# Graph attention with routed experts: the feed-forward and routing stage written out without a loop, weight splitting moved to POOL in the attention

## What is computed

```
hs = layer_norm(_layernorm(x)); ht = layer_norm(h_target)
q = (ht @ Wq + bq) / sqrt(32); k = hs @ Wk + bk; v = hs @ Wv + bv      # 8 heads
logits = where(adj != 0, q @ k.T, -1e30); probs = softmax(logits)
ht = layer_norm(ht + (probs @ v) @ Wo + bo)
x = x + ht + gelu(ht @ W1) @ W2                                          # W1: 256x1024
xn = _layernorm(x); gate_logits = xn @ gate_w.T
vals, idx = top_k(gate_logits, 2); topk_w = softmax(vals)
for e in range(8):                                                       # 8 experts, 256->1024->256
    x += comb[:, e:e+1] * (gelu(xn @ w1[e].T + b1[e]) @ w2[e].T + b2[e])
```

## Time and profile before

| What | Value |
|---|---|
| Median of 3 runs (lowest, highest) | 1286.0 us (1283.02, 1286.46) |
| The profiled execution: time, span | 1281.83 us, 1279.9 us |
| Mean granted clock of TensorE, share of full speed | 0.903 |
| Busy, share of the span: PE, ACT, DVE, POOL | 81%, 63%, 63%, 14% |
| Moved by DMA | 128.71 MB, mean 101 GB/s |

### The profile page before, as it was taken

How to read it: one execution, slowest core, us unless ns; L and a number is a source line. 1 busy time by engine, 2 the same in 40 slices (tenths; PEclk the granted TensorE clock), 3 DMA queues, 4 the chain that set the end, 5 groups by cost and what they waited for, 6 DMA issues and landing times. The chain is left out here.

```text
span 1279.9 us, 25331 instructions
## 1 busy us (share of the span) xinstructions
PE 1030.5 (81%) x7150; PEld 638.6 (50%) x7151; DVE 802.6 (63%) x2186; ACT 804.0 (63%) x975; POOL 181.0 (14%) x163
## 2 busy tenths in 40 slices
PE   4926699989999899989999258558612899999994
PEld 2612244444444444444444135345411788888984
DVE  7718477867787677867787268838851534433442
ACT  4514599989999899889988125325402655555552
POOL 6400000000000000000000121331241122222221
PEclk9965699999999999999999569969955999999997
DMA  5693313311151113211240734253235232333323
GB/s 173 155 317 109 119 51 117 116 44 40 50 178 51 50 51 113 97 52 50 86 145 29 260 105 165 80 185 135 85 110 187 80 52 51 51 51 51 51 49 84
DMA packets 84561, 128.71 MB, mean 101 GB/s; under 512 B 16283, under 2 KB 59043, under 8 KB 81731
## 3 DMA queue, kind: packets, MB, share of 16 engines
q1 hardware_dynamic: 71954, 115.06, 27.9%
q0 software_dynamic: 8656, 11.29, 5.3%
q10 hardware_dynamic: 3856, 1.19, 0.4%
HBM read 96.82 MB, written 26.23 MB: 96 GB/s over the span
## 5 line engine op out<-in xcount | busy, mean ns | idle before, releaser
L597 DVE CUSTOM_DVE_ANT_0 masked<-ps,maskA 128x512 f32<-128x512 f32 x544 | 366.4, 690 | 125.4 <-PE ps L699 105.2
L699 PE MATMUL ps<-ks,qs 96*128 96x512 f32 x544 | 267.2, 533 | 62.0 <-DVE piecemax L597 28.9
L652 ACT ACTIVATE masked<-masked,negmax 128x2048 f32<-128x2048 f32 x135 | 270.4, 2003 | 53.5 <-DVE negmax L603 50.1
L677 ACT ACTIVATE weights<-ps 128x1024 f32<-128x1024 f32 x256 | 254.0, 1015 | 38.4 <-PE ps L721 35.8
L719 PE MATMUL ps<-qs,ks 98*128 98x512 f32 x514 | 234.6, 515 | 6.7 <-DMA qs<-shift_lo 3.4
L721 PE MATMUL ps<-maskB,identb 128*128 (+1 forms) x514 | 205.1, 399 | 0.0
L699 PEld LDWEIGHTS ps<-ks,qs 96*128 96x128 f32 x544 | 109.4, 201 | 137.6 <-DVE piecemax L597 78.0
L1643 DVE TENSOR_TENSOR gT<-wall,gT 128x2048 f16<-128x2048 f32 x25 | 57.3, 2293 | 148.6 <-ACT gT L1697 148.6
L1736 PE MATMUL ps<-xT,wall 128*128 128x256 f16 x1200 | 139.7, 278 | 9.8 <-DVE xT L1634 9.8
L731 PE MATMUL ps<-weights,v_all 128*32 128x256 f32 x2048 | 137.1, 385 | 0.0
L1736 PEld LDWEIGHTS ps<-xT,wall 128*128 x1200 | 119.1, 100 | 26.5 <-issue 10.4
(11 more groups left out here) (178 smaller groups left out, 1046.4 us busy)
## 6 DMA issues: line engine op xcount, KB each, us to landing
adjA<-in_adj SPq DMA_DIRECT2D x20, 1024.0 KB, 5.9
adjB<-in_adjT SPq DMA_DIRECT2D x40, 512.0 KB, 4.1
wst<-in_w1T SPq DMA_DIRECT2D x8, 1024.0 KB, 4.8
wst<-in_w2T SPq DMA_DIRECT2D x8, 1024.0 KB, 5.6
xr<-expert_rows SPq DMA_DIRECT2D x26, 272.0 KB
qs<-q_high SPq DMA_DIRECT2D x70, 64.0 KB, 2.0
ks<-kq_hi SPq DMA_DIRECT2D x32, 128.0 KB, 2.3
wall<-ctx_cols SPq DMA_DIRECT2D x6, 512.0 KB
```

The lines of the kernel that those rows point to most:

```text
L597: dve.tensor_tensor_reduce(masked[:, a % 2, k * 512:(k + 1) * 512], ps[:, u % 2, :], maskA[:, a, k * 512:(k + 1) * 512], 1.0, NO_EDGE, ALU ...
L652: act.activation(masked[:, a % 2, :], masked[:, a % 2, :], ACT.Exp, bias=negmax[:, h % 2, a:a + 1], accum_out=rowsum[:, h % 4, a:a + 1]).t ...
L677: act.activation(weights[:, j % 4, :, :], ps[:, 2 + 2 * (j % 2):4 + 2 * (j % 2), :], ACT.Exp).then_inc(weights_ready, 1)
L699: pe.matmul(ps[:, u % 2, :], qs[0:KR, h % 4, a * P:(a + 1) * P], ks[0:KR, h, k * 512:(k + 1) * 512], start=True, stop=True)\
```

## The change

- Block 1 also writes a table of padding rows (`pad_rows`) to memory, and issues the attention's first two mask loads (`adjA`) before its barrier.
- In the attention POOL now works. In each head's step it divides one context by its sums (`scale_context`, on 64x256), splits one quarter of a 256x1024 pair of weights with three operations on 128x1024 (`split`), stores the halves to memory (`split_weights`), loads the next quarter, and copies `pad_rows` two or three times into `expert_rows`, so that every expert's region is full of padding beforehand. DVE inverts the sums of each head (`invert_sums`, 128x4, at u = 8). SP stores these inverses (`store_sums`), loads them spread over partitions (`load_inv`), and stores the context (`store_context`) behind the shift, once POOL has scaled it.
- Block 3 is written out for its four blocks, with no loop. No float32 weights are split in it: the halves are loaded in sets (`load_set`). ACT applies the normalisations (`normalise`), POOL adds the bias of the projection to the rows ahead of time (`add_bias`), DVE works on 128x512 and 128x1024 at once, `hidden` runs over all eight f first, and `back` follows for two tiles of 128 rows at a time. The hidden layer has a buffer for each of two blocks. There is no padding at its end, and the sets of the last experts are loaded as their memory comes free.
- Block 4 splits no weights.

```diff
                     def store_context(n, b, h):
-                        wait_apart(sp, context_summed, n + 2)
+                        wait_apart(sp, context_scaled, n + 2)
...
                     def store_sums(n, h):
-                        wait_apart(sp, rowsum_ready, TPB * (n + 1))
-                        sp.dma_start(sums[:, bass.ds(n, 1), :], rowsum[:, h % 4, :]).then_inc(sums_out[h % 4], 16)
+                        wait_apart(sp, inv_ready, n + 1)
+                        sp.dma_start(inv_rows[bass.ds(n, 1), :].rearrange("o (a p) -> p (o a)", p=P),
+                                     rowsum[:, h % 4, :], allow_slow_non_contiguous=True).then_inc(sums_out[h % 4], 16)
+                    def load_inv(n, b, h):
+                        sp.wait_ge(sums_out[h % 4], 16 * (b * (H // 4) + h // 4 + 2))
+                        sp.wait_ge(context_scaled, n + 1)
...
+                    def split(i):
+                        wait_apart(pool, wch_in, 16 * i + 16)
+                        pool.tensor_scalar(wch[:, :], wch[:, :], WSCALE, None, ALU.mult).then_inc(wch_scaled, 1)
...
+                        pool.tensor_copy(whl[:, 0, :], wch[:, :]).then_inc(wch_split, 1)
...
+                        pool.tensor_tensor(whl[:, 1, :], wch[:, :], whl[:, 0, :], ALU.subtract).then_inc(wch_split, 1)
...
+                    with pool.Fori(0, NB) as b:
+                        for h in range(H):
+                            n = b * H + h
+                            if h:
+                                scale_context(n - 1, h - 1)
+                            split(n + 4)
+                            store_split(split_weights[bass.ds(e + 1, 1), h // 2 % 2, :, :, h % 2, :]
...
+                                load_expert(2 * b + (h + 1) // 4, h + 1)
...
+                            for i in range(2 * (h % 4), 2 * (h % 4) + (3 if h % 4 == 3 else 2)):
+                                prefill(bass.ds(e * REGION + i * PR, PR))
+                        scale_context(n, h)
...
+                            elif u == 8:
+                                invert_sums(n + 1, (h + 1) % 4)
...
-                        dve.wait_ge(g_high, FC * b + f + 1)
-                        dve.tensor_tensor(gT[:, 1, f % 2, :], g32[:, f % 2, :], gT[:, 0, f % 2, :], ALU.subtract)\
+                        dve.wait_ge(g_high, FC * b + f + 1)
+                        dve.tensor_tensor(gT[b % 2][:, 1, f, :], g32[:, f % 2, :], gT[b % 2][:, 0, f, :],
...
-                    for n in range(2):
-                        stage_high(act, 0, n)
-                    high_turned(0, 0)
+                    normalise_h(0)
+                    high_turned(0)
+                    normalise_h(1)
+                    normalise_h(2)
+                    for f in range(FC):
+                        hidden_high(0, f)
+                        if f == 5:
+                            normalise_h(3)
...
+                    scatter(0)
+                    row_factors(1, 2)
+                    scatter(1)
+                    row_factors(1, 3)
+                    scatter(2)
+                    scatter(3)
```

More of the change, by code:

```diff
@@ L91, in graph_attention_and_experts @@
         ks = sb("ks", [KR + 2, H, T], F32R, ph12)
+        adjA = sb("adjA", [P, 2, T], I32, ph12)
+        adj_t = adj.rearrange("(i p) s -> i p s", p=P)
+        adjA_in = [sem(f"adjA_in{i}") for i in range(2)]
         x_in = [sem(f"x_in{g}") for g in range(NG)]
@@ new lines, in scatter @@
+                    def scatter(b):
+                        pool.wait_ge(rows_ready, 2 * b + 2)
+                        pool.wait_ge(slots_ready, 2 * b + 2)
+                        for a in range(TPB):
+                            for k in range(TOPK):
+                                pool.indirect_dma_start(
+                                    out=expert_rows[:, :], in_=rows[:, b % 2, a, :], in_offset=None,
+                                    out_offset=bass.IndirectOffsetOnAxis(ap=slots[:, b % 2, k, a:a + 1], axis=0),
+                                    bounds_check=E * REGION - 1).then_inc(scattered[b % 2], 16)
@@ new lines, in _ @@
+                    pe.wait_ge(wo_in, 16)
+                    attention_out(0)
+                    attention_out(1)
+                    turn_h2(0)
+                    attention_out(2)
+                    pe.wait_ge(ffn_in, 32)
+                    hidden(0, 0)
+                    attention_out(3)
+                    for f in range(1, FC):
+                        hidden(0, f)
+                    turn_h2(1)
+                    for f in range(FC):
+                        hidden(1, f)
+                    back(0, 0)
@@ new lines, in _ @@
+                    back(0, 1)
+                    turn_h2(2)
+                    for f in range(FC):
+                        hidden(2, f)
+                    back(1, 0)
+                    turn_xn(0)
+                    back(1, 1)
+                    pe.wait_ge(gw_in, 16)
+                    gates(0)
+                    turn_h2(3)
+                    for f in range(FC):
+                        hidden(3, f)
+                        if f == 4:
+                            pe.wait_ge(c3_ready, 8)
+                            ranks(0)
@@ L1543, in graph_attention_and_experts @@
+                    back(2, 0)
+                    turn_xn(1)
+                    back(2, 1)
+                    gates(1)
+                    back(3, 0)
+                    ranks(1)
+                    back(3, 1)
+                    turn_xn(2)
+                    gates(2)
+                    ranks(2)
+                    turn_xn(3)
+                    gates(3)
+                    ranks(3)
         ph4 = ExitStack()
@@ L1704, in _ @@
                     middle(0, 0)
-                    for n in range(2):
-                        stage_high(act, LATE[1], n)
                     with act.Fori(0, NPAIR // 2) as jj:
```

960 lines of the change are left out of this document (465 added, 495 removed).

## The result

The changed kernel takes 1447.6 us (median of 4 runs, 1445.3 to 1459.5), the kernel before beside it 1286.2 (4 runs). The ratio is 1.128, interval 1.122 to 1.134. The profiled execution has a span of 1445.2 us against 1279.9. The forecast was 1224, with a range up to 1262: both the sign and the size were wrong.

A forecast was written before the change was run, and what follows sets the result against it. It took PE (539 of 578 us) and ACT (517) as close to full in the attention. -14 - 49 - 5.5 - 11.5 + 21.5 = -58.5 from 1281.83 gave 1223.3, forecast 1224 us; range 1198 to 1262.

The forecast's parts named there:

- The attention pays: Attention: what the change costs there through its start, POOL's work, DVE's reciprocal, locks and transfers, +21.5 us in sum.
- (a): Attention's start: adjA loads queue ahead of the queries and the barrier awaits the padding's store; +2.5 us, bounds -4.8 to +4.8.
- (e): Attention's transfers: POOL's added traffic makes adjB late; +6 us, bounds 0 to 20 (0.6 in each of 32 heads).
- (c): Attention, DVE's reciprocal on 128x4: short, any wait fits DVE's 3.9 us standing still a head; costs nothing.
- (d): Attention, DVE beside POOL: masks wait for POOL's operations, mask-and-maximum never; 10 us over the blocks plus 3 ahead of the loop.
- last shift to first `hidden`: Head of block 3: the sums' transpose store, reload and POOL's product go; 37.5 us against 51.8, -14 us.
- body: Block 3's feed-forward and routing between head and tail: walked at 122 us against 170.7, -49 us.
- tail: End of feed-forward and routing, set by POOL's scatters: 38 us from PE's last `back` against 43.5, -5.5 us.
- start of the experts: Experts' first products, no longer waiting for a late weight: second product at 986.5 instead of 998.06, -11.5 us.
- (b): Attention, POOL's work a head: 10.6 us, at worst 16.2, below the head's 16.57, so POOL follows.
- Rival 2: Attention: every head pays, by late adjB or DVE waiting for POOL; +32 to +54 us, about 1250 us; chance 0.20.
- Rival 4: Attention: POOL's series outlasts the head and sets the pace, slower in the end; about 1301 us; chance 0.07.

The follow-up runs named there:

- 16-byte kernel without weights: Changed kernel with the reciprocals' store in 16-byte pieces, and without the experts' weights' load, split and store in the attention's loop: 1220.2 us, ratio 0.948.
- 16-byte kernel: Changed kernel with the reciprocals' store in 128 pieces of 16 bytes instead of 512 of 4, contexts scaled by other rows' reciprocals: 1292.9 us, ratio 1.006.

## Why the prediction was wrong, step by step

**The step that failed first is a store that is not in the sum.** Under "The attention pays" stand (a) to (e), and none is the store of the reciprocals. In (c) I priced the reciprocal on DVE, "nothing", and not the transfer that carries its result, one line ahead of the shift on SP's queue. The old store of the sums stood at the same place, so I counted it as unchanged; its form had changed. The evidence that it would matter was in the diff, in the rearrangement and in `allow_slow_non_contiguous=True`. No row of the trace of before had a store in 4-byte pieces; it should then have been bounded from both sides, and as PE waits for the shift in every head, each late microsecond is paid 32 times. What the runs showed in place of nothing: the store lands in 10.2 us, PE waits 166.1 us in 32 heads for the shift behind it, and in all it costs 146 to 155 us here and 180 in the kernel before.

The last shift of the attention dates the loss, one row each of before, the 16-byte kernel without weights, the 16-byte kernel, and the changed kernel:

```profile
697.12 0.62 SPq L488 DMA_DIRECT2D qs<-shift_hi  x1
```

```profile
716.15 0.62 SPq L522 DMA_DIRECT2D qs<-shift_hi  x1
```

```profile
791.50 0.62 SPq L522 DMA_DIRECT2D qs<-shift_hi  x1
```

```profile
937.48 0.62 SPq L522 DMA_DIRECT2D qs<-shift_hi  x1
```

| term | forecast, us | measured, us | from |
|---|---|---|---|
| the 4-byte store | not priced | +146 | 937.48 - 791.50 |
| experts' weights, split and moved | (d) +13 and most of (e)'s +6 | +75 | 791.50 - 716.15 |
| all else in the attention | (a) +2.5 and the rest of (e) | +19 | 716.15 - 697.12 |
| last shift to first `hidden` | -14 | -11 | 47.0 against 57.7 |
| body | -49 | -50 | 121.0 against 170.7 |
| tail | -5.5 | +2 | 45.5 against 43.5 |
| start of the experts | -11.5 | -14 | 14.9 against 29.1 |

The rows of the changed kernel behind the last four are its windows above and these, the first `hidden` and the first two products of the experts:

```profile
984.44 0.81 PE L1497 MATMUL ps<-wall 128*128 128x512 f16 x3
...
1157.83 7.74 PE L1768 MATMUL ps<-xT,wall 128*128 128x256 f16 x48
...
1165.84 4.42 PE L1768 MATMUL ps<-xT,wall 128*128 128x256 f16 x39
```

The terms sum to 146 + 75 + 19 - 11 - 50 + 2 - 14 = 167; the spans differ by 165.3, the rest being the experts behind their second product, 279.4 us instead of 281.8. The split between the first two lines is that of one order of removal; the two together are shown. The third line was undersized too: without any weights in the loop the attention still loses 19 us. Of these 3.5 stand ahead of the first shift, 4.6 in the first step (48.2 us against 43.6) and 6.6 in the first two heads of the later blocks and the second of the first; what holds these I did not separate.

**(a) Start, +2.5.** The first shift came at 115.65 instead of 112.21, +3.4. Right.

**(b) POOL follows, 10.6 us a head.** Right in the sum. L619, L623, L625 and L638 take 2.79, 1.06, 2.17 and 0.73 us, the issues some 2.9: about 9.7. POOL idled 452.7 us ahead of L638. My 1.2 for the first operation of the split was too low and the 2.94 I bounded it by was near; the two-input one came at 2.17 instead.

**(c) The reciprocal, nothing.** Right for DVE (0.173 us), and the step where the transfer behind it was overlooked.

**(d) Locks, +13.** Right in kind. L723 has a mean of 689 ns against 690, so the mask-and-maximum was never lengthened. The masks did, seldom (a group by line, and a row of the view of tile adjB):

```profile
L683 DVE TENSOR_SCALAR maskA<-adjA 128x2048 bf16<-128x2048 int32 x20 | 26.1, 1307 | 1.6 <-DMA adjA<-in_adj 1.6
```

```profile
L689 DVE TENSOR_SCALAR maskB<-adjB x39: 687/691/2614, 129.9 to 931.4; 128x1024 int32 x32, 128x1024 bf16<-128x1024 int32 x7
```

20 x 0.085 us for `mask_a`, and a median of 0.69 with a longest of 2.61 for `mask_b`: a few microseconds, not 13.

**(e) Transfers, +6, "since POOL's transfers start after its split, mostly past the shift's".** The mechanism was right, and the run without the split work shows that the shift was indeed spared that way. The size was off by more than a factor of ten: the weights cost 75 us. The transfer that paid was adjB, which I had named: in the 16-byte kernel 57.8 us in 22 waits instead of 13.8 in 9, and 19.0 without the weights. I took 6 of a bound of 20; the bound itself (0.6 us a head, from one late adjB) was too low. It took the lateness seen with a DMA share of 0.25, where the attention of the 16-byte kernel has 0.46; that this is the reason is argued, from adjB's landing of 4.1 us there and 5.4 here.

**The range.** The recorded text gives 1212 to 1240 as what follows from the bounds of (a) to (e). Its own bounds, all taken at once, give 1197 to about 1276. The result lies far outside both.

**Block 3.** The body came as walked, 121.0 us for 122. The head came near only in its sum. From the block's first row to the first `hidden` it took 27.1 us (957.35 to 984.44) where I had 32.5, but from the last shift to that row 19.9 us, where it had been 8.5 before (697.12 to 705.65) and I had added 2.5. Two errors of opposite sign made -11 out of my -14; that is luck. The tail failed: it shortened nothing. `scatter` waited 3.47 and 6.94 us for DVE's slots where I had 5.4 in all, and from the issue of its last of 32 at 1145.17 to the barrier at 1150.9 it took 5.7 us where I had 2 of landing.

**Rivals.** Rival 2 (adjB late in every head) comes nearest to what the kernel with 16-byte pieces does, with 22 waits and at 69 us above the forecast, more than the 32 to 54 I gave it. No rival had the store of the reciprocals. Rival 4 had the sign and a wrong cause: POOL never set the pace.

## What to carry over

A store or load whose last dimension is strided must be priced by its pieces, even if it moves 2 KB: ask what is in flight beside it on any queue, since in both of the other places tried here it only found another victim. Where a change adds transfers to a stage whose transfers are just in time, first issue those a stage earlier, if their buffer is free, and then add. A repeated transfer with a changed access pattern counts as a new one.

## What the runs showed of the hardware that I had not expected

- 512 pieces of 4 bytes take 8.9 to 10.2 us to land (medians), 128 pieces of 16 bytes 1.4 to 3.4 us for the same 2 KB. While they were in flight, SP's issue of two 64 KB loads on another queue took 9.26 us instead of 0.80, and the DMA engines moved 7 GB/s with some 1.5 MB of POOL's waiting. The busy share of the engines shows none of it: 0.20 in the attention that lost most of 186 us to them, 0.25 before.
- A reciprocal on DVE costs by the row's length: 173 ns for 128x4, 935 ns for 4x128, 953 ns for 128x128, where a cast of 4x128 takes 275 ns in the changed kernel (L696).
- Leaving out six microseconds of POOL's arithmetic a head made the kernel 37 us slower. That arithmetic had been holding 1.6 MB of transfers back from the shift; the wait for the shift grew by 21 us, and the rest is not explained.
